# Order of the openings in a four-layer graph network's feed-forward parts: gated outputs, last tile's split and feature sums

## The reference, cut to what matters

```python
h = jnp.maximum(_layernorm(x), 0.0)               # 1024 nodes x 512
h = (h - mu) * rsqrt(var + EPS) * bn_w + bn_b
h = gcn(h, src, dst, gcn_in_w, gcn_in_b)          # graph convolution
for i in range(4):
    a = attn(ln(h, ln2_w[i], ln2_b[i]), cond, Wq[i], Wk[i], Wv[i], Wo[i])
    h = h + a
    u = ln(h, ln3_w[i], ln3_b[i]) @ geglu_w[i] + geglu_b[i]     # 512 -> 4096
    val, gate = split(u, 2)
    f = val * gelu(gate)                                        # 2048 wide
    h = h + f @ ffo_w[i] + ffo_b[i]
out = x + gcn(h, src, dst, gcn_out_w, gcn_out_b) + h_in
```

## Time and profile before

| what | value |
|---|---|
| median of 3 runs | 2414.64 us (2413.85 to 2414.74) |
| the profiled execution | 2411.93 us |
| its span in the profile | 2410.1 us |
| PE busy | 2361.3 us, 98% of the span |
| DVE, ACT, POOL busy | 69%, 46%, 28% |
| chain that ended last | PE 89%, DVE 7%, ACT 2% |
| granted TensorE clock, mean | 0.994 |

### The profile page before, as it was taken

The page is one execution under the profiler, slowest core; times in us unless marked ns, Lnnn a source line. Parts: engine busy times, 40 slices in busy tenths (PEclk is TensorE's granted clock), DMA queues, the critical chain, the costliest instruction groups (busy, mean ns, idle before and its releaser), DMA issues.

```text
span 2410.1 us, 32870 instructions
## 1 busy us (share of the span) xinstructions
PE 2361.3 (98%) x12039; PEld 1959.3 (81%) x12039; DVE 1653.6 (69%) x3184; ACT 1115.3 (46%) x2198; POOL 666.3 (28%) x439
## 2 busy tenths in 40 slices
PE   6889999999999999999999999999999999999999
PEld 5448888888888888878888888888888888878887
DVE  8986767675566767775566766775566766775554
ACT  8964444554334444554334444554334444554332
POOL 3011000066541000066541000066540000066540
PEclk8999999999999999999999999999999999999999
DMA  2031001122211101112111101122211100122222
GB/s 79 18 127 40 36 18 35 36 62 76 65 66 36 36 18 36 36 62 78 62 66 36 36 18 36 36 62 79 63 64 36 35 21 33 36 65 76 66 108 80
DMA packets 83307, 125.00 MB, mean 52 GB/s; under 512 B 5904, under 2 KB 63888, under 8 KB 78288
## 3 DMA queue, kind: packets, MB, share of 16 engines
q1 hardware_dynamic: 82864, 118.75, 15.0%
q10 hardware_dynamic: 288, 4.19, 0.4%
HBM read 116.36 MB, written 6.55 MB: 51 GB/s over the span
## 4 chain that ended last, share of the span: by engine, by line
PE 89%; DVE 7%; ACT 2%; issue 1%; POOL 0%; DMA 0%; SPq 0%; DVEq 0%; ACTq 0%; POOLq 0%
PE ps L2018 19%; PE ps L2019 19%; PE ps L2020 19%; PE ps L2348 7%; PE ps L2352 7%; PE ps L2350 7%; PE ps L2256 2%; PE ps L2273 2%; PE ps L2275 2%; DVE oh_d L1496 1%; PE ps L2270 1%; PE ps L2546 1%; DVE w_lo L1881 1%; DVE z L1876 1%; ACT z L1017 1%
## 5 line engine op out<-in xcount | busy, mean ns | idle before, releaser
L618 POOL TENSOR_TENSOR rstd<-veps,mhalf 128x1 f32<-128x1 f32 x48 | 28.8, 600 | 893.0 <-DVE veps L1287 893.0
L719 POOL TENSOR_TENSOR f_lo<-ff,f_hi 128x512 fp32r<-128x512 f32 x128 | 166.7, 1312 | 166.3 <-ACT f_hi L1176 166.1
L1949 DVE TENSOR_TENSOR h<-h,ps 128x512 f32<-128x512 f32 x256 | 168.7, 683 | 63.1 <-PE ps L2020 62.5
L968 ACT ACTIVATE v_hi<-ps 128x512 fp32r<-128x512 f32 x128 | 76.7, 599 | 285.5 <-PE ps L2020 285.5
L2018 PE MATMUL ps<-cond_hi,w_hi 128*128 128x512 f32 x512 | 202.1, 395 | 0.0
L2018 PE MATMUL ps<-w_hi,cond_hi 128*128 128x512 f32 x512 | 200.8, 392 | 0.0
L2020 PE MATMUL ps<-w_hi,cond_lo 128*128 128x512 f32 x512 | 200.3, 391 | 0.0
L2019 PE MATMUL ps<-cond_lo,w_hi 128*128 128x512 f32 x512 | 200.1, 391 | 0.0
L2020 PE MATMUL ps<-cond_hi,w_lo 128*128 128x512 f32 x512 | 200.1, 391 | 0.0
L2018 PE MATMUL ps<-wf_hi,f_hi 128*128 128x512 f32 x512 | 199.6, 390 | 0.5 <-DVE ff L1933 0.5
L2019 PE MATMUL ps<-w_lo,cond_hi 128*128 128x512 f32 x512 | 199.9, 390 | 0.0
(11 more groups left out here) (324 smaller groups left out, 6487.8 us busy)
## 6 DMA issues: line engine op xcount, KB each, us to landing
stage<-in_pieces SPq DMA_DIRECT2D x82, 512.0 KB, 3.3
stage<-in_condT SPq DMA_DIRECT2D x31, 1024.0 KB, 4.7
stage<-in_pieces SPq DMA_DIRECT2D x224, 128.0 KB, 2.6
at_s<-at_hi ACTq DMA_DIRECT2D x2, 2048.0 KB, 7.6
at_hi<-at_s SPq DMA_DIRECT2D x4, 1024.0 KB, 6.4
x<-in_x SPq DMA_DIRECT2D x2, 1024.0 KB, 6.9
out<-h SPq DMA_DIRECT2D x8, 256.0 KB, 2.0
bias_row<-in_rows SPq DMA_DIRECT2D x6, 256.0 KB, 3.6
```

What stands on the lines that cost most here:

```text
L719: pool.tensor_tensor(f_lo[q % 2][:, c, half * HALF:(half + 1) * HALF], ff[:, s % 2, :], bits(f_hi[q % 2][:, c, half * HALF:(half + 1) * HA ...
L1949: dve.tensor_tensor(h[:, t, :], h[:, t, :], ps[:, down_bank(q, t), :], ALU.add)\
```

## The change

Four calls move, one in ACT's list and three in DVE's, and none is added. In ACT's list of each layer, the high part of the third feature sum (part 0) goes from before the last tile's high part to behind the second gelu. In DVE's list, the third feature sum goes from before `z3_of(NT - 1)` to behind the first lower part; `x3_low(NT - 1)` goes ahead of the second feature sum, which then stands directly ahead of `mlp_step(1)`; and `mlp_step(3)` goes from behind the three lower parts of part 1 and `add_bias` to directly behind `weight_sums(1, 1)`.

```diff
                 a21_high()
-                t_high(3, 0)
                 x3_high(7)
                 f_high(0, 0, 0, 0)
                 gelu(1)
+                t_high(3, 0)
                 t_high(2, 0)
...
                 residual(NT - 1, norm0 + ln3_index(NT - 1))
-                t_sums(0, (3,))
                 z3_of(NT - 1, norm0 + ln3_index(NT - 1))
                 mlp_step(0)
                 t_low(1, 0)
+                t_sums(0, (3,))
+                x3_low(NT - 1)
                 t_sums(0, (2,))
-                x3_low(NT - 1)
                 mlp_step(1)
...
                 weight_sums(1, 1)
+                mlp_step(3)
                 for n in (1, 3, 2):
                     t_low(n, 1)
                 add_bias(NT - 1)
-                mlp_step(3)
                 t4_low()
```

## The result

| what | before | after |
|---|---|---|
| median of 16 runs each | 2413.39 us (2411.11 to 2415.84) | 2418.38 us (2416.21 to 2421.36) |
| ratio, after to before | | 1.0019, 95% interval [1.0012, 1.0026] |
| the profiled execution | 2411.93 us | 2416.33 us |
| its span | 2410.1 us | 2414.5 us |
| granted TensorE clock, mean | 0.994 | 0.993 |

The account below looks back on a forecast made before the run. PE, busy 98% of the span, was taken to bound the kernel. Layers 1.42 + 0.67 + 1.42 + 1.35 made +4.9 us, giving 2419.5 us; the forecast's own range was 2418 to 2421.5, the wider one 2414.5 to 2423.5.

Parts of the forecast that it names:

- Nothing for the sum ahead of the normalisation: Moving the third sum leaves L1817 at 493.79 and the 1.7 us of PE waits in the openings: 0.
- The 0.54: The feature sum behind L1817 makes POOL's subtraction 0.54 late; alternation carries it on, so L1902 ends at 509.06, not 508.52.
- The rival without it: POOL gets the turn ahead of the feature sum, so the 0.54 doesn't happen: +2.7, 2417.3 us; chance 0.08.
- The gain at 514.81: PE's wait for the fourth gated output goes in each opening: 3.4 us plus 4 x 0.08 for the slow first matmul.
- The turns: Behind the fourth gated output, DVE and POOL alternate; full_set(0) starts at 519.49 in place of 517.91, 1.58 late.
- What comes back: At set (2, 0) the earlier load and PE's small stall give some back, leaving +1.42 for the first layer.
- the loss at 1072.67: In the second layer the load landed late and PE lost 0.6; the earlier load gives that back.
- the hitch: In the fourth layer full_set(0) was 0.37 late already; +1.22 if that goes, +1.55 if it stays, 1.35 taken.
- The near tie: Second-set weight sum (about 533.70) against POOL's subtraction (533.72): POOL's turn taken; were DVE to win, the sum is 3.8.
- a fall in every layer: TensorE's clock falls some 3.5 us near 520, costing 1.7 a layer: +11.7, 2426 us; chance 0.05.
- POOL is not in the way: full_set(0) is ready before PE wants it and the gain stays whole: -4 to -6.4, 2408 to 2410.5; chance 0.06.
- the split comes late: POOL's next-layer weight split comes after 515.3, so bias and L1886 go first: -2.5, 2412 us; chance 0.04.

Follow-up runs that it names:

- The first experiment: The change with the fourth gated output put back behind the lower parts and the bias, sums still moved: 2415.97 us, ratio 1.0009, +2.3 us to before.
- The kernel with the split later: The change with POOL's split of the next layer's weights moved behind the low part of full_set(0)'s output: 2425.03 us, ratio 1.0042 to before.
- the order by turns: The kernel before with the fourth gated output between part 1's first and second lower parts, and the bias behind set_first(1, 1): 2406.59 us, ratio 0.9967.
- more idle: The change with one unused DVE sum over 1024 columns added ahead of full_set(0) in each layer: 2424.83 us, ratio 1.0042 to before.
- third sum only: The kernel before with only the third feature sum moved behind the first lower part and its high part behind the second gelu: 2413.61 us, ratio 0.9999.

## Why the prediction was right

The time, the sign and the mechanism came out as forecast; the chances were divided evenly over the line of 0.2%, and the ratio is 1.0019, on it. The forecast of +4.9 stands beside a measured +5.0, but that is closer than its terms deserve, as the part on the clock shows. The 1.1 between 2419.5 and 2418.38 is the base: it was the median of three runs, 2414.64, and the 16 runs have 2413.39.

1. **Nothing for the sum ahead of the normalisation.** Right: L1817 is at 493.79 on the scale, 1.8 us of waits have stayed, and the kernel with that move alone is at 0.9999.
2. **The 0.54.** Right to a hundredth: the sum lasts 0.95, POOL's subtraction 2.98, L1902 ends 0.54 late. The first experiment shows it by itself, as 0.53 at `full_set(0)` and +2.3 us. The rival without it (0.08) falls.
3. **The gain at 514.81.** Right: that wait is gone.
4. **The turns.** The ends were computed as 511.01, 513.54, 514.98 and 517.55 for POOL and 518.09 for the bias. Measured, less the opening's 0.12, POOL ends at 511.01, 513.55, 514.99 and 517.54 and the bias at 518.09. The *mis-sized term* is the one behind it: "L1886 at 519.38, and `full_set(0)` starts at 519.49". L1886 took 1.21 and not 1.37, so it ended at 519.23; and `full_set(0)` started 0.07 before that end and not 0.11 behind it, since its gelu was long ready. It starts at 519.16, so 1.25 late and not 1.58, and the edge of set (2, 0) moves by 1.04 and not 1.42. One line over the span shows the duration, against the earlier trace rows:

```profile
L1886 DVE TENSOR_TENSOR xT_lo<-z,xT_hi x4: 1209/1211/1214, 518.1 to 2145.5; 128x1024 fp32r<-128x1024 f32 x4
```

The prediction read the 1.37 wrong when it said that L1886 "found POOL idle". In the kernel before L1886 starts at 516.43, and POOL's low part of the gated output runs from 515.41 to 516.71. L1886 was waiting for a turn: by the prediction's own rule it reads from 516.57 and lasts 0.14 more than 1.21, 1.35. It is 1.36 to 1.37 in all four layers of each of the three kernels in which POOL ends 0.28 behind its start, and 1.21 in the four in which POOL has ended before it. That DVE stood idle ahead of it is not the reason, as a subtraction of the same shape shows, with POOL idle and after an idle of DVE:

```profile
516.43 1.37 DVE L1886 TENSOR_TENSOR xT_lo<-z,xT_hi 128x1024 fp32r<-128x1024 f32 x1 [1.76 <-ACT xT_hi L1169]
...
200.19 1.23 DVE L1393 TENSOR_TENSOR cond_lo<-stage,cond_hi 128x1024 fp32r<-128x1024 f32 x1 [0.37 <-ACT cond_hi L796]
```

5. **What comes back.** Right in kind: `weight_sums(2, 0)` no longer waits for its load and L1897 lasts 2.60, as forecast; PE's small stall near 530 is gone. In the second layer the earlier load gave back the loss at 1072.67, as forecast. Layer by layer, +1.03, +0.36, +1.12 against the forecast's +1.42, +0.67 and +1.42, each 0.3 to 0.4 below, which is the mis-sized term. The fourth layer, less its clock fall, has +0.81 against +1.35: there `full_set(0)` is at 519.16 as in the others, so the hitch went, the case that the prediction had at +1.22.

**The near tie.** The later weight sum, L1897 at 533.47, again lasts 1.57 and not about 0.4: POOL had the turn, the case I took. The Trainium skill's rule that the shared pair is exclusive ("SBUF — State Buffer", "Who interferes with whom") agrees with the runs throughout: the bias is 0.68 without POOL's split and 2.90 with it. Of who wins, that section of the Trainium skill says that issue order decides, and, where it speaks of DVE's two-port modes, that the first issued keeps the pair for its whole instruction. The recorded starts do not bear that out at a near tie. The ten traces hold 36 such ties of L1897 with POOL's L719, with starts within 0.04 us of each other; DVE's is the earlier one in 21, and DVE waited in all 36, lasting 1.52 to 1.61 in place of 0.41. Whether the recorded start is the moment of issue, no run here shows.

**The clock.** I gave 0.05 to a fall in every layer. It was neither that nor nothing: a fall in one layer of four in the profile, worth about 0.95 (a rival in the prediction had it at 1.7). The sum of the layers without it is 3.3, below my 4.9, and with it and the start's 0.12 it is the 4.4 of the spans. So the closeness of +4.9 to +5.0 is luck in part, errors of opposite sign: a path taken 0.3 to 0.5 per layer too long, 1.5 in all, and a clock taken as steady. The medians' 5.0 is 0.6 above the spans' 4.4. The profiled execution, at 2416.33, is the second fastest of the 16, and the three slowest runs have mean clocks of 0.990 and 0.991 against its 0.993; I read the 0.6 as more clock falls in the usual run, which the profile of one run cannot show. It stays open: the part ahead of the first opening, with clock falls of its own, takes between 490.6 and 493.0 us in the ten profiled executions, and that spread alone would cover 0.6.

**The rivals** "POOL is not in the way" and "the split comes late" fall with the bias at 2.90. The kernel with the split later does not price the second at its 2412: that rival lets the split follow L1886, and the experiment puts it behind `full_set(0)`, where it ends at 522.09 in place of 520.08 and the load behind it comes too late. Nearer to the rival is the order by turns, with the split behind L1886, at −7.1.

## What to carry to other kernels

When an early result is placed ahead of a queue, ask what it wakes on the other engines: here the gated output came 5 us sooner, POOL's low part of it and the split behind that ran some 2 us sooner, took turns ahead of DVE's, and cost more than the wait that went. Two engines that take turns are best ordered as one list, with the long instruction of the one set against what the other can spare; the fourth gated output moved one place less far, with the sums left alone and the bias out of the way, gave −8.4 us in place of +5.0. And where an instruction is put off, look at what stands behind its new place: the bias taken out of one critical path stood in the next one, until it was put behind that as well.

## What the hardware showed that I had not expected

- TensorE's clock fell to 1.2 GHz, mostly for 3.4 us, right behind waits of about 2.0 us in one layer of four and of 3.1 us in three of four, though in the kernel before a full clock followed an idle of 3.39 us. The other kernels have falls behind waits of 1.83, 1.97, 2.93 and 3.02 and none behind waits of 2.52 and 3.29, nor behind any of 1.71 or less there. So a wait on PE can cost more than its length, and by how much differs from layer to layer: a fall of 3.4 us put the next edge back by 0.95 to 1.0 in the change and with more idle, and by an estimated 1.1 to 1.6 in three other kernels.
- The last part of the load for set (2, 0) landed 4.5 to 5.5 us behind the end of POOL's split in 38 of the 40 layers traced, and 6.6 and 7.0 us behind it in two, the second layers of "third sum only" and of the order by turns. There PE waited 1.57 and 1.83.
- The same subtraction of 128x1024 on DVE took 1.21 with POOL idle, 1.23 with POOL idle and after an idle of DVE, and 1.36 where it started 0.28 ahead of the end of one of POOL's. A DVE that stood still first is no proof that an instruction had the port to itself.
